# Gathering transposed attention weights with 512 KB DMAs instead of 128 KB ones, keys in another order

## The reference

```
xn  = layernorm(x)                               # 32 x 256 x 128
h   = layernorm(xn) * ln_scale + ln_bias         # inside the attention
c_q, c_kv = h @ w_down_q.T, h @ w_down_kv.T      # 64 latents per token
q, k, v   = up projections of c_q, c_kv, c_kv    # 16 heads of 64
q, k      = rotary embedding of q, k
attn      = softmax(q @ k.T / 8)                 # 256 x 256 per head
out       = (attn @ v) @ w_out.T + xn
result    = x + out + spikes(relu(xn @ W_fc.T)**2 @ W_proj.T)
```

## Time and profile before

| | before |
|---|---|
| time, median of 3 runs | 1033.13 us (1032.72 to 1034.09) |
| profiled execution, its own time | 1031.75 us |
| its span, first to last instruction | 1030.0 us |
| TensorE busy | 990.9 us, 96% of the span |
| ScalarE / VectorE / GpSimd busy | 89% / 88% / 87% |
| matmuls | 6880 instructions |
| DMA traffic | 217.96 MB, mean 212 GB/s |
| DMAs of the moves | 1020 on SP and 4 on ScalarE, 128 KB each |

### The profile page before, as it was taken

One profiled execution on the slowest core, in us unless ns is written; L12 is line 12 of the kernel. 1 busy time (PEld: TensorE's weight loads), 2 busy tenths in 40 slices (PEclk: granted clock), 3 DMA queues, 4 the chain that ended last, 5 costly groups with the idle time before them and its releaser, 6 DMA issues.

```text
span 1030.0 us, 25979 instructions
## 1 busy us (share of the span) xinstructions
PE 990.9 (96%) x6880; PEld 732.6 (71%) x6880; DVE 907.0 (88%) x1223; ACT 914.3 (89%) x3007; POOL 895.2 (87%) x898
## 2 busy tenths in 40 slices
PE   4689999999999999999999999999999999999997
PEld 3566777777777777777777777777777777777765
DVE  4898899999999999999999989999999999998972
ACT  4789899999999999999999999999999999999872
POOL 4878989999989999999998999999898999998862
PEclk9899999999999999999999999999999999999999
DMA  6578888888887888888788887888888788888873
GB/s 190 149 215 220 205 220 229 221 216 219 227 211 219 211 217 221 223 215 220 212 217 219 232 206 219 221 208 220 224 216 219 219 210 219 221 211 226 221 184 91
DMA packets 93281, 217.96 MB, mean 212 GB/s; under 512 B 22464, under 2 KB 43200, under 8 KB 93120
## 3 DMA queue, kind: packets, MB, share of 16 engines
q1 hardware_dynamic: 92896, 216.00, 78.8%
q10 hardware_dynamic: 352, 1.57, 0.7%
HBM read 7.77 MB, written 4.19 MB: 12 GB/s over the span
## 4 chain that ended last, share of the span: by engine, by line
PE 80%; issue 6%; DVE 5%; POOL 4%; ACT 2%; SPq 1%; DMA 1%; DVEq 0%; ACTq 0%; POOLq 0%
PE ps_s L353 20%; PE ps_u L369 19%; PE ps_b L474 10%; PE ps_qk L341 7%; PE ps_a L410 5%; PE ps_qk L342 5%; PE ps_a L423 5%; PE ps_b L440 3%; PE ps_a L382 2%; POOL partner L1010 2%; POOL qk L1013 2%; DVE latent L858 1%; ACT prob L614 1%; DVE turned L830 1%; DVE qk L813 1%
## 5 line engine op out<-in xcount | busy, mean ns | idle before, releaser
L614 ACT ACTIVATE prob<-ps_s,neg_max 128x256 f32<-128x256 f32 x1024 | 478.4, 501 | 21.7 <-DVE neg_max L818 19.4
L1010 POOL TENSOR_TENSOR partner<-partner,rope_sb 128x512 f32<-128x512 f32 x256 | 327.4, 1279 | 46.5 <-DMA partner<-raw 46.1
L830 DVE STREAM_TRANSPOSE turned<-prob 128x1024 f32<-128x1024 f32 x256 | 316.8, 1238 | 38.7 <-ACT prob L614 37.3
L1013 POOL TENSOR_TENSOR qk<-qk,partner 128x512 f32<-128x512 f32 x256 | 327.0, 1277 | 20.1
L818 DVE TENSOR_REDUCE neg_max<-ps_s 128x4 f32<-128x1024 f32 x256 | 310.5, 1213 | 18.2 <-PE ps_s L353 13.6
L353 PE MATMUL ps_s<-qk 64*128 64x256 f32 x2048 | 267.6, 395 | 7.1 <-ACT prob L614 4.1
L369 PE MATMUL ps_u<-gathered,ckv 128*64 128x256 f32 x2048 | 249.3, 385 | 1.6 <-DMA gathered<-turned 0.9
L614 ACT ACTIVATION_READ_ACCUMULATOR prob<-ps_s,neg_max 128x1 f32 x1024 | 237.7, 232 | 0.0
L353 PEld LDWEIGHTS ps_s<-qk 64*128 64x128 f32 x2048 | 185.2, 187 | 53.1 <-POOL qk L1013 15.6
L369 PEld LDWEIGHTS ps_u<-gathered,ckv 128*64 128x64 f32 x2048 | 135.6, 136 | 80.5 <-issue 9.9
L813 DVE TENSOR_TENSOR qk<-ps_qk,rope_sb 128x512 f32<-128x512 f32 x246 | 165.4, 672 | 20.9 <-ACT raw L626 19.3
(11 more groups left out here) (85 smaller groups left out, 925.6 us busy)
## 6 DMA issues: line engine op xcount, KB each, us to landing
gathered<-turned SPq DMA_DIRECT2D x1020, 128.0 KB, 2.3
partner<-raw SPq DMA_DIRECT2D x256, 256.0 KB, 2.4
x_sb<-in_x SPq DMA_DIRECT2D x32, 128.0 KB, 2.1
resid<-early SPq DMA_DIRECT2D x32, 128.0 KB, 2.0
out<-out_sb SPq DMA_DIRECT2D x32, 128.0 KB, 2.0
turned<-in_wup ACTq DMA_DIRECT2D x2, 512.0 KB, 6.0
rope_sb<-in_rope SPq DMA_DIRECT2D x1, 512.0 KB, 6.9
turned<-in_wo_t SPq DMA_DIRECT2D x1, 512.0 KB, 7.5
```

The costliest lines, as they stand in the source:

```text
L614: last = nc.scalar.activation(prob[:, s % 2, :, h, :, t, :].rearrange("p j k c -> p k j c"), ps_s[:, s % 2, h, t, :].rearrange("p (k j c) ...
L830: nc.vector.transpose(turned[:, par, :, s % GROUP, :], prob[:, s % 2, :, :, :, :, :].rearrange("p j h k t c -> p j (h k t c)"))\
L1010: nc.gpsimd.tensor_tensor(other, other, sin_sb, ALU.mult).then_inc(sin_ready, 1)
L1013: nc.gpsimd.tensor_tensor(qk[:, s % RING, :, :], qk[:, s % RING, :, :], other, ALU.add).then_inc(rope_done, 1)
```

## The change

`move` issues one DMA for a row of blocks instead of four: its source is all four key blocks of 32 partitions, its destination all 128 partitions of `gathered`. The elements are taken in order, so source partition c with blocks j = 0 to 3 fills the destination partitions 4c + j. A key at place c of block j thus lies on partition 4c + j instead of 32j + c. So that `ckv` has the same order, `copy_inputs` writes token 128t + 32j + c to column 128t + 4c + j of `h_t`, and `latents` reads `h_t` back in the old order, at a step of four elements. `weigh_latents` and `turn` wait for a quarter of the counts. Bytes moved, matmuls and their shapes stay.

```diff
+        def by_row(tokens):
+            return tokens.rearrange("d (t c j) -> d t j c", t=TT, j=Q)
...
                 for rows in rows_of:
-                    for block_of in range(Q):
-                        sp.dma_start(gathered[32 * block_of:32 * block_of + 32, par, rows, :, :, :, :, :],
-                                     turned[32 * rows:32 * rows + 32, par, block_of, :, :]).then_inc(moved[par], 16)
+                    sp.dma_start(gathered[:, par, rows, :, :, :, :, :].rearrange("p g h k t r -> p (g h k t r)"),
+                                 turned[32 * rows:32 * rows + 32, par, :, :, :].rearrange("p j g s -> p j (g s)"))\
+                        .then_inc(moved[par], 16)
...
-                    pe.wait_ge(moved[(s // GROUP) % 2], (i * (BODY // GROUP // 2) + s // GROUP // 2 + 1) * 16 * Q * Q)
+                    pe.wait_ge(moved[(s // GROUP) % 2], (i * (BODY // GROUP // 2) + s // GROUP // 2 + 1) * 16 * Q)
...
-                nc.tensor.matmul(ps_a[:, 0:S], wdown_sb[:, :], h_t[:, par, :], start=True, stop=True).then_inc(cc_ready, 1)
+                nc.tensor.matmul(ps_a[:, 0:S], wdown_sb[:, :], by_row(h_t[:, par, :]), start=True, stop=True)\
+                    .then_inc(cc_ready, 1)
...
-                nc.scalar.activation(h_t[:, par, :], ps_a[:, 0:S], ACT.Identity, bias=ln_sb[:, 1:2], scale=ln_sb[:, 0:1])
+                nc.scalar.activation(by_row(h_t[:, par, :]), ps_a[:, 0:S].rearrange("d (t j c) -> d t j c", t=TT, j=Q),
+                                     ACT.Identity, bias=ln_sb[:, 1:2], scale=ln_sb[:, 0:1])
...
-                for block_of in range(Q):
-                    act.dma_start(gathered[32 * block_of:32 * block_of + 32, par, rows, :, :, :, :, :],
-                                  turned[32 * rows:32 * rows + 32, par, block_of, :, :]).then_inc(moved[par], 16)
+                act.dma_start(gathered[:, par, rows, :, :, :, :, :].rearrange("p g h k t r -> p (g h k t r)"),
+                              turned[32 * rows:32 * rows + 32, par, :, :, :].rearrange("p j g s -> p j (g s)"))\
+                    .then_inc(moved[par], 16)
```

More of the change, by code:

```diff
@@ L827, in turn @@
                 if s % GROUP == 0 and not outside(g - 2 * GROUP, STEPS):
-                    dve.wait_ge(moved[par], (i * (BODY // GROUP // 2) + s // GROUP // 2) * 16 * Q * Q)
+                    dve.wait_ge(moved[par], (i * (BODY // GROUP // 2) + s // GROUP // 2) * 16 * Q)
                     dve.sem_inc(dve_waited, 1)
```

## The result

The changed kernel takes 1088.01 us (median of 4 runs, 1084.74 to 1090.00) against 1032.93 us before in the same runs: a ratio of 1.0532, 95% interval 1.0501 to 1.0563. The forecast was 1030.7 with a range of 1027 to 1045: wrong in sign and far outside. The case that came true is the second rival, moves that become slower until DMA sets the pace, to which I had given 0.12.

The account below looks back on a forecast made before the run. TensorE was taken as its own bound in the steady stage. Lead-in −1.0, tail −1.4 and steady stage 0 gave −2.4 us on the profiled 1031.75, so 1029.35; with the median 1.38 above, 1030.7 us, range 1027 to 1045.

Parts of the forecast that it names:

- second rival: Steady batches: moves become slower and DMA the bound, 1092 us at 13 us per move, some 1540 at half rate; chance 0.12.
- price of the move: DMA queues: the new move was taken to run at the old move's 205 GB/s, 10.1 us.
- other price in the prediction: DMA move: by the Trainium skill's port rule a source of 32 partitions stays at 218 GB/s, 9.6 us.
- SP's pace: Old move: a reading that SP's issuing sets its rate, 128 KB in 0.63 us, 208 GB/s.
- Lead-in and tail: Both ends of the run: earlier exchanges win 1.0 us in the lead-in, fewer waits win 1.4 us in the tail.
- third rival: Moves become fast, 5.6 us; lead-in −3.1 and tail −2.4 give 1027.6 us; chance 0.08.
- SP's issue: SP's queue: four issues per move cost some 2 us, freeing SP 8 us earlier; by itself worth nothing.
- write side: ScalarE's write of h_t at a step of 16 bytes: even a doubling, +0.56 us, ends in idle time; 0.
- read side: TensorE's latents matmul reading h_t at a step of 4 elements: taken as 0, high end 48 us in all.
- first rival: Strided read slows the latents matmul, at half speed +0.43 us per batch, 13.8 us in all, 1044.5 us; chance 0.30.

Follow-up runs that it names:

- reordered moves: Changed kernel with the four transfers of each move issued in the order 0, 2, 1, 3: 1054.22 us, ratio 1.0200.
- sixteen spread transfers: Sixteen 128 KB transfers from every fourth to every fourth partition, timed alone behind the end of the kernel before: 209 GB/s at a DMA share of 0.53.
- fast moves: Changed kernel with h_t in the old order and four 512 KB moves from all 128 to all 128 partitions: 1028.74 us, ratio 0.9963.

## Why the prediction was wrong, point by point

**The step that failed** is the price of the move: "I take 205 GB/s, 10.1 us, as the row of the old move is nearest: half of its pattern, the source, stays." By itself the new move takes 12.18 us at 172 GB/s. In the kernel a batch of 32.41 us, less 6.7 for the other transfers, leaves 12.9 us for a move if the queues are the bound throughout; the 0.7 us between the two, and the same in the reordered moves, are not explained by a run. Nor was the other price in the prediction, 9.6 us, reached. Two faults led there. I put the rate of the old move down to its partitions, and rejected SP's pace by the share of 0.91; sixteen spread transfers show the same rate at 0.53, so the row is no measure of what the partitions allow. And half a pattern isn't a price: with the same 128 partitions at the receiving end, one transfer took 4.57 or 1.55 us by where its 32 sources lay.

**The second rival** had the mechanism ("the engines that share a destination order crowd on few source partitions"), the point from which it decides (12.0 us per move) and, at 13 us, 1092 us; 1088 was measured. It got 0.12 because "reads and writes of 32 partitions together already run at 205", the same misread row. What I gave as its sign, a weighing that waits for `gathered`, was wrong: moves have time in hand and exchanges hardly any, so the wait appears at GpSimd, ScalarE and the scores.

**Lead-in and tail** (−1.0 and −1.4). With slow moves both went the other way: GpSimd's wait for partner in 0 to 125 us rose from 12.9 to 18.9 us, and the tail lost 8.7 us.

```profile
POOL partner L1015 <- DMA partner<-raw: 18.9, 6, 7.3
```

With fast moves of the same number the kernel won 3.5 us, where the third rival had 5.5 from the two ends.

**SP's issue** (four issues in 2 us): 7.38 us in the kernel, and 3.20 even with the fast moves of 128 to 128 partitions. The row was of a single load in the prologue.

**The write side** (0): right, 1.0002. **The read side** (0): wrong in size, 3.4 us, four times less than the first rival's 13.8. The Trainium skill's rule that an access to another line of 16 bytes each time pays (Advanced Engine Details and Errata, SBUF Cachelines) agrees in sign with the matmul's 483 to 664 ns. In the changed kernel this cost can't be told apart from the waits. It alone is more than the 2.4 us that the whole forecast hoped to win, and about what the fast moves won, 3.5 us; the two together were not run.

**Two figures of the prediction** don't match one another: 2.10 MB at 205 GB/s are 10.2 us, not 10.1, and −0.5 to −4 us from 1033.13 is 1029.1 to 1032.6, not 1028.5 to 1032.5. Nothing hangs on either.

## What to carry to other kernels

Price a transfer by a row with the same partitions at both ends; a neighbour with one end the same can be off by a factor of two (5.35 and 12.18 us to the same 128 partitions), and fewer, larger DMAs were not faster here, where each read 32 adjacent partitions. Add up the DMA time of a stage before changing a transfer in it: at 26.9 of 30.7 us this one had room for 1.9 us per move by the sum, and in fact for less, as the reordered moves show: 1.3 us longer than the old ones by themselves (11.55 against 10.28), they cost 2%. What was late here was the transfer with the least slack, the exchange, and not the one that had grown.

## What the runs showed of the hardware

A transfer of 512 KB from 32 to 128 partitions took 4.58, 2.69 and 1.57 us as its sources lay 1, 2 and 4 partitions apart, and 2.1 MB from 128 to 32 adjacent partitions took 17.16 us, three times as long as from 128 to 128. Why the distance counts is not shown. How long SP issues depends on the transfers as well: four of 512 KB took it 7.38 us from 32 to 128 partitions and 3.20 us from 128 to 128. And extra DMA work of 2.7 us a batch (an estimate from 5.35 us for four such transfers alone), in a kernel whose batches already held 26.9 us of it by the prediction's sum, cost 1%; 5.4 us cost 6.4%.
